# Graph network kernel: 832 record gathers move from the loop ahead of attention into the attention stage

## What is computed

```
edge_index = jnp.stack([src, dst])
x = _layernorm(x + _L0_gnn_ref(x, edge_index, ...))                  # attention over the edges, 4 heads
x = _layernorm(x + _L1_gnn_ref(x, node_vec1, W, b, edge_index))      # masked, degree-weighted sums
x = _layernorm(x + _L2_gnn_ref(x, edge_weight, edge_attr_3, ...))    # radial, equivariant messages
x = _layernorm(x + _L3_gnn_ref(x, edge_index, W1, b1, W2, b2))       # two graph convolutions
```

## Time and profile before

| | us |
|---|---|
| median of 3 runs (20086.42 to 20103.31) | 20091.59 |
| span of the profiled execution | 25995.0 |
| the profiled execution's own time | not in the page |
| DVE busy in the span | 16714.1 (64%) |
| POOL busy in the span | 13429.9 (52%) |
| PE busy in the span | 9853.2 (38%) |
| ACT busy in the span | 6288.5 (24%) |

### The profile page before, as it was taken

How to read it: one execution, slowest core, us unless ns; L and a number is a source line. 1 busy time by engine, 2 the same in 40 slices (tenths; PEclk the granted TensorE clock), 3 DMA queues, 4 the chain that set the end, 5 groups by cost and what they waited for, 6 DMA issues and landing times.

```text
span 25995.0 us, 290953 instructions
## 1 busy us (share of the span) xinstructions
PE 9853.2 (38%) x63545; PEld 7350.7 (28%) x63546; DVE 16714.1 (64%) x23622; ACT 6288.5 (24%) x13799; POOL 13429.9 (52%) x14067
## 2 busy tenths in 40 slices
PE   0131000000000006765225666666666666324422
PEld 0131000000000006664223444444444444313421
DVE  9898574547344438888555666666666677555555
ACT  0002121112111105543002333333333345201400
POOL 0187676667777760000664555555555552363165
PEclk6555555555555559985556777777777776555555
DMA  1133434441000001116222000000000006424623
GB/s 14 25 33 27 29 31 29 29 29 13 6 6 6 6 15 48 41 52 227 69 69 18 9 10 9 9 9 9 9 9 9 9 10 144 137 64 87 205 65 61
DMA packets 1751558, 1095.98 MB, mean 42 GB/s; under 512 B 1217323, under 2 KB 1658124, under 8 KB 1750028
## 3 DMA queue, kind: packets, MB, share of 16 engines
q0 software_dynamic: 454272, 412.11, 13.3%
q1 hardware_dynamic: 1089532, 417.46, 6.8%
q10 hardware_dynamic: 207632, 265.14, 3.3%
HBM read 700.94 MB, written 391.12 MB: 42 GB/s over the span
## 4 chain that ended last, share of the span: by engine, by line
DVE 31%; another core or an unknown queue 21%; issue 17%; DVEq 12%; PE 11%; ACT 4%; DMA 2%; ACTq 1%; POOL 0%; SPq 0%; POOLq 0%
PE banks L1423 5%; DVE arena L1768 5%; DVE arena L1767 4%; DVE red L2523 4%; DVEq L2201 3%; DVE hot L2196 2%; DVE arena L1740 2%; DVE arena L2207 2%; DVE srcs L2516 2%; PE banks L1365 2%; PE banks L1410 2%; DVEq L498 1%; DVE arena L1585 1%; DVEq L2261 1%
## 5 line engine op out<-in xcount | busy, mean ns | idle before, releaser
L804 POOL DMA_INDIRECT srcs<-spread,nbx x2808 | 2653.2, 945 | 5691.9 <-issue 3372.8
L782 POOL DMA_INDIRECT gat<-tab,nbr x3328 | 3455.0, 1038 | 2537.8 <-issue 1271.9
L1423 PE MATMUL banks<-w2rows,dsts 128*128 128x384 f32 x6656 | 3443.8, 660 | 1030.2 <-DVE srcs L2516 699.0
L782 POOL DMA_INDIRECT gat<-tab,pay x3328 | 3161.6, 950 | 1077.4 <-issue 892.0
L748 POOL DMA_INDIRECT pay<-records,nbr x2560 | 2746.2, 1073 | 843.1 <-issue 827.1
L1208 PE MATMUL banks<-ident,arena 128*128 128x128 f32 x2240 | 436.2, 379 | 7154.4 <-DVE arena L1768 2837.8
L909 ACT COPY banks<-arena 128x1024 f32<-128x1024 f32 (+1 forms) x1508 | 1318.6, 875 | 6430.8 <-issue 2701.9
L2511 DVE TENSOR_TENSOR srcs<-banks,g_s 128x512 f32<-128x512 f32 x1664 | 1146.1, 689 | 2252.6 <-remote 1505.1
L1208 PEld LDWEIGHTS banks<-ident,arena 128*128 128x128 f32 x2240 | 400.7, 204 | 7190.5 <-DVE arena L1768 2844.2
L2523 DVE TENSOR_REDUCE red<-srcs 128x160 f32<-128x2560 f32 x832 | 2346.2, 2820 | 75.6
L1279 PE MATMUL banks<-srcs,hot 128*128 128x96 bf16 (+1 forms) x11232 | 1169.8, 281 | 3175.7 <-DVE hot L2196 2136.8
(11 more groups left out here) (392 smaller groups left out, 22029.8 us busy)
## 6 DMA issues: line engine op xcount, KB each, us to landing
spread<-srcs SPq DMA_DIRECT2D x936, 192.0 KB, 2.9
dsts<-key_rows SPq DMA_DIRECT2D x234, 512.0 KB, 4.1
spread<-srcs ACTq DMA_DIRECT2D x468, 204.0 KB, 2.4
staged<-gat SPq DMA_DIRECT2D x416, 148.0 KB
gat<-staged ACTq DMA_DIRECT2D x416, 148.0 KB, 2.1
dsts<-key_rows ACTq DMA_DIRECT2D x117, 512.0 KB, 4.3
gat<-tab,nbr POOLq DMA_INDIRECT x3328
gat<-tab,pay POOLq DMA_INDIRECT x3328
```

Of the source, the lines that this page charges most:

```text
L782: pool.indirect_dma_start(out=gatv(s, GC[pas])[:, t, :], out_offset=None, in_=TAB[pas], in_offset=bass.IndirectOffsetOnAxis(ap=row, axis=0 ...
L804: pool.indirect_dma_start(out=chunk_rows(s, c)[:, q, :], out_offset=None, in_=rows, in_offset=bass.IndirectOffsetOnAxis(ap=nbx[:, r, s * X ...
L1423: last = t_.matmul(bank[1 + 2 * (p % 2) + h][:, 0:384], hid_rows[:, s % 2, 2 * p + h, :], w2rows[:, :], start=True, stop=True)
```

## The change

POOL's first record loop covers 54 rounds instead of 80 (`EARLY_ITERS` = 54, 1728 gathers). The next 26 rounds (`MID_ITERS`, 832 gathers) are made by a new loop, `mid_records`, of 104 rounds with four steps, two gathers a step, into the small buffer `late`. Each pair waits for its indices, for its slot and for the logits of the attention step with its number. SP has a loop of its own for them, `mid_loads`. The counts behind them are raised to match; the radial layer takes the same 24 rounds as before.

```
+MID_ITERS = 26
+MID_TILES = 2
+READY_ITERS = ITERS - LATE_ITERS
+EARLY_ITERS = READY_ITERS - MID_ITERS
...
+            def mid_round(i, first, final):
+                for s in range(SLOTS):
+                    if not first:
+                        sp.wait_ge(rec_in[s], i * (16 * MID_TILES) + 16 * TPS * EARLY_ITERS)
+                        sp.dma_start(by_dst_v[:, mid_tiles(i - 1, s), :], late[:, s, :, :]).then_inc(rec_out[s], 16)
+                    if not final:
+                        sp.dma_start(nbr[:, s, 0:MID_TILES], ids_dst[:, mid_tiles(i, s)]).then_inc(nbr_in[s], 16)
+
+            def mid_loads():
+                mid_round(0, True, False)
+                with sp.Fori(1, ITERS) as i:
+                    mid_round(i, False, False)
+                mid_round(ITERS, False, True)
...
             record_loads()
+            mid_loads()
             chunk_number_loads(PASS_L1, from_dst)
             send_table(1, tab2, F)
             for s in range(SLOTS):
-                sp.wait_ge(rec_out[s], 16 * EARLY_ITERS)
+                sp.wait_ge(rec_out[s], 16 * (EARLY_ITERS + ITERS))
             edge_loads()
...
+            def mid_records():
+
+                def step(i, s):
+                    pool.wait_ge(nbr_in[s], nbr_count(1, EARLY_ITERS + i))
+                    pool.wait_ge(rec_out[s], i * 16 + 16 * EARLY_ITERS)
+                    pool.wait_ge(logit_ready, i * SLOTS + (s + 1))
+                    pool.nop(nofuse=True)
+                    for t in range(MID_TILES):
+                        pool.indirect_dma_start(
+                            out=late[:, s, t, :], out_offset=None, in_=records,
+                            in_offset=bass.IndirectOffsetOnAxis(ap=nbr[:, s, t:t + 1], axis=0),
+                        ).then_inc(rec_in[s], 16)
...
             gather(PASS_MAX)
             collect()
+            mid_records()
             chunk_gather(0, PASS_L1, C1, spread[0])
```

More of the change, by code:

```diff
@@ L42 @@
 LATE_ITERS = 24
-EARLY_ITERS = ITERS - LATE_ITERS
+MID_ITERS = 26
+MID_TILES = 2
+READY_ITERS = ITERS - LATE_ITERS
+EARLY_ITERS = READY_ITERS - MID_ITERS
 LATE_TILES = 2
@@ L75 @@
 assert LATE_ROUNDS * LATE_TILES == LATE_ITERS * TPS
-assert EARLY_ITERS < LATE_ROUNDS < ITERS and LATE_ITERS * SLOTS + 1 < LATE_ROUNDS + SLOTS
+assert MID_ITERS * TPS == ITERS * MID_TILES and MID_TILES == LATE_TILES
+assert READY_ITERS < LATE_ROUNDS < ITERS and LATE_ITERS * SLOTS + 1 < LATE_ROUNDS + SLOTS
 assert XROWS * M == CHUNKS * CHUNK_EDGES and QROWS * M == P * NT and XGPS * XTILES == TPS
@@ L599, in record_loads, with mid_tiles @@
                 record_round(EARLY_ITERS, False, True)
+            def mid_tiles(i, s):
+                return bass.ds(i * (SLOTS * MID_TILES) + (EARLY_ITERS * SLOTS * TPS + s * MID_TILES), MID_TILES)
+            def mid_round(i, first, final):
[10 more added lines that the diff above has]
+                mid_round(ITERS, False, True)
             def late_tiles(i, s):
-                return bass.ds(i * (SLOTS * LATE_TILES) + (EARLY_ITERS * SLOTS * TPS + s * LATE_TILES), LATE_TILES)
+                return bass.ds(i * (SLOTS * LATE_TILES) + (READY_ITERS * SLOTS * TPS + s * LATE_TILES), LATE_TILES)
             def edge_round(i, late_store, late_load, first=False, late_step=None):
@@ L608, in edge_round @@
                     if late_step is not None:
-                        due = late_step * 16 + 16 * (EARLY_ITERS + s + 1)
+                        due = late_step * 16 + 16 * (EARLY_ITERS + ITERS + s + 1)
                         if not isinstance(i, int):
@@ L621, in edge_round @@
                     if late_store:
-                        sp.wait_ge(rec_in[s], i * (16 * LATE_TILES) + 16 * TPS * EARLY_ITERS)
+                        sp.wait_ge(rec_in[s], i * (16 * LATE_TILES) + (16 * TPS * EARLY_ITERS + 16 * MID_TILES * ITERS))
                         sp.dma_start(by_dst_v[:, late_tiles(i - 1, s), :], late[:, s, :, :]).then_inc(rec_out[s], 16)
@@ L628, in edge_loads @@
                 edge_round(0, False, True, True)
-                with sp.Fori(1, EARLY_ITERS) as i:
+                with sp.Fori(1, READY_ITERS) as i:
                     edge_round(i, True, True)
-                with sp.Fori(EARLY_ITERS, LATE_ROUNDS) as i:
-                    edge_round(i, True, True, late_step=i * SLOTS - EARLY_ITERS * SLOTS)
-                edge_round(LATE_ROUNDS, True, False, late_step=(LATE_ROUNDS - EARLY_ITERS) * SLOTS)
+                with sp.Fori(READY_ITERS, LATE_ROUNDS) as i:
+                    edge_round(i, True, True, late_step=i * SLOTS - READY_ITERS * SLOTS)
+                edge_round(LATE_ROUNDS, True, False, late_step=(LATE_ROUNDS - READY_ITERS) * SLOTS)
                 with sp.Fori(LATE_ROUNDS + 1, ITERS) as i:
-                    edge_round(i, False, False, late_step=i * SLOTS - EARLY_ITERS * SLOTS)
+                    edge_round(i, False, False, late_step=i * SLOTS - READY_ITERS * SLOTS)
             def neighbour_load(i, s):
@@ L755, in collect @@
                     step(i, False)
+            def mid_records():
[9 more added lines that the diff above has]
+                        ).then_inc(rec_in[s], 16)
+                for s in range(SLOTS):
+                    step(0, s)
+                with pool.Fori(1, ITERS) as i:
+                    for s in range(SLOTS):
+                        step(i, s)
             def late_records(i, s, first):
-                pool.wait_ge(nbr_in[s], nbr_count(1, EARLY_ITERS + i))
-                if not first:
-                    pool.wait_ge(rec_out[s], i * 16 + 16 * EARLY_ITERS)
+                pool.wait_ge(nbr_in[s], nbr_count(1, EARLY_ITERS + ITERS + i))
+                pool.wait_ge(rec_out[s], i * 16 + 16 * (EARLY_ITERS + ITERS))
                 pool.nop(nofuse=True)
```

## The result

The changed kernel takes 20164.53 us (median of 5 runs, 20157.94 to 20171.1) beside 20086.66 us for the kernel before in the same session (5 runs, 20077.45 to 20103.31): a ratio of 1.0039, 95% interval 1.0028 to 1.005. It is slower by 78 us, more than the 0.2% that can be told from no change. The forecast was no change; the time lies inside the range that was given.

What follows compares the result with a forecast made beforehand. The prediction took attention to be bound by DVE, with POOL's record gathers done 458 us before they are wanted. Its terms summed to 0 us on the path, so 20091 us, range 19900 to 20200.

Steps and rivals of the forecast that it cites:

- Are the waits beside gathers in the runs?: DVE's waits beside POOL's gathers in the stretched profile: claimed to be mostly absent from the runs.
- The rivals that held the waits for real: Waits real: attention takes them, 20593 to 20740 us, chance 0.07; or it does not, 19325 to 19500, chance 0.20.
- the sum of 5998 against 5903: Waits before attention, in radial and chunk gather stages: 5998 us, against 5903 us by which the profiled execution exceeds a run.
- The timeline of a run: Start to first chunk gather: attention from 6428, POOL's last record gather at 8520, chunk gathers wanted at 8978.
- 458 us of slack: Before the first chunk gather: POOL is done with its record gathers 458 us before it is wanted.
- 832 gathers behind the logits: 0 us: Moved pairs on POOL's queue: logits always ready, gathers issued at the same moments, ending at 8520; 0 us.
- Loop rounds: 67 us, covered: POOL's new loop: 78 more rounds at 0.86 us, 67 us, covered by the 458 us, of which 391 remain.
- Buffers: 9.0 us against a round of 9.96: A slot's pair in the new loop: 9.0 us until its next pair can follow, within a 9.96 us round; costs nothing.
- The 14.4 us a round: Time per round of the new loop above which POOL would be late for the chunk gathers, wanted at 8978.
- SP and later stages: 0: SP's 832 DMAs take at most 582 us of 1036; the radial stage fetches the same last 24 iterations; 0 us.
- The rival that came true: POOL late for the chunk gathers, small rounds paid: 20159 us, or 20262 at 16 us per round; chance 0.13.
- The profile after: Profiled span of the changed kernel: between 25230 and 26640 us, thought 26300, while the runs stand still.

Runs made afterwards that it cites:

- e1: The kernel before, with no edit, profiled a second time: span 20097.7 us in an execution of 20099.57 us, median of its runs 20082.47 us.
- e2: The changed kernel without POOL's wait for the logits in the moved gathers: 20161.59 us, ratio 1.0044 to the kernel before.
- e5: The changed kernel with the moved gathers in rounds of four tiles a slot, 52 rounds in place of 104: 20079.92 us, ratio 1.0003 to the kernel before.
- e7: The changed kernel with its two record loops in the other order and no wait for the logits: 20104.66 us, ratio 1.0014 to the kernel before.

## Why the prediction was wrong

- **Are the waits beside gathers in the runs?** Right. e1 keeps DVE busy for 4325 of 4541 us beside the neighbour gathers, and attention starts at 6277. The rivals that held the waits for real (20593 to 20740, and 19325 to 19500) had nothing. But the sum of 5998 against 5903 only said that the parts fit as a whole; it was no check of POOL's pace. The rule that records cost no cycles, from which I took what speaks for those rivals ("NOTIFIC — the notification-queue block", section 10, of the Trainium skill), is not contradicted by e1: its profiled execution took 20099.57 us, and the runs beside it 20065.99 to 20101.24. It doesn't explain, and no run here does.
- **The timeline of a run: the step that failed.** "POOL starts at 1189 and needs 5888 x 1.245 = 7331 us: its last record gather is at 8520." It is at 9030, 510 us later. The neighbour gathers took 1.36 us each, not 1.245 (381 us for 3328), the records 1.289 (111 us for 2560), and 17 us lie between the two. I had taken 0.944 us from the radial stage's records, where nothing else uses much of the DMA engines. The row of the stretch itself has 6200.73 us for 5888 gathers: 1.053 each, and with 0.30 between them 1.353; that sum ends at 9156, past the 8978 at which I had the chunks wanted. It is a row of the stretched execution, and in e1 the same gathers are busy for 6030.4 us; but the evidence that there was no cover stood in a row that I had used only for its count. The other end was off as well: attention came at 6277 and not 6428, and DVE was ready at 8787 and not 8978. In place of 458 us of slack there were 250 us of lateness (458 - 510 - 191, and the wait for the chunk numbers).
- **832 gathers behind the logits: 0 us.** Right that the wait never holds (1.2 us; e2). Wrong that the first loop ends at 7484 (7903.5); the pairs met the end of attention and the spread stage, not attention.
- **Loop rounds: 67 us, covered.** Wrong twice: nothing covered them, and they are next to nothing. A turn costs at most 0.14 us (e5), 11 us for 78 of them, and none is to be seen in e7's 500 us. The 0.86 us of the earlier trace rows was one turn in the stretched execution; in e1 the longest idle time of that kind ahead of a record gather is 0.3 us.
- **Buffers: 9.0 us against a round of 9.96.** Right in quiet stretches (177 gathers in 220 us). In the spread stage it was 14.5 us in the turn shown and 12.9 on average, where POOL's own work for a round is 11.1. "The taken value is 9.0, and it costs nothing" is the second step that failed: the landing time of the earlier trace rows was carried into a stage at 226 GB/s. This term, which I held to be nothing, is the 78 us: in that stage POOL is idle for 221.7 us ahead of 445 gathers, 86 us more than the 0.30 us before each; e5 removes it by giving the chain twice the time. The 14.4 us a round at which I had the rival decide counted on the slack; without it every round above POOL's own pace is paid.
- **SP and later stages: 0.** Right: SP's DMA instructions are 0.35 us each, and the radial stage needs 14.1 us a step in both (5874 and 5853 us for 416), against the 14.2 worked out.
- **The rival that came true** is POOL being late for the chunk gathers, at 0.13 and 20159 us; measured 20164.53. Its place is right and its price right by luck: it has the 67 us of loop turns, and the time was lost to landings. Its chance of 0.13 did not reckon with how little it took: 1.245 us a gather where the mean is 1.33, 7% more, used up all of the slack.
- **The profile after.** Wrong: I expected a span near 26300 from a stretched execution, and 20165.4 came.

The Trainium skill's page "SBUF — State Buffer", section "Who interferes with whom", has a DVE instruction with two SBUF inputs contend with a GpSimd instruction that reads SBUF. That bears on the term that failed: beside such instructions gathers took 1.41 us (below). The prediction had asked of them only whether DVE slows, and not whether POOL does.

## What to carry over

Where an engine makes 5888 equal steps, its pace has to be read in the very stretch in which it runs: take the row's own busy time and gap for one step, multiply them out to the end, and only then speak of slack. Where the bound is one in-order queue, moving work within that queue wins nothing; moving it past the instruction that others wait for wins its full length (32 gathers 40 us, 96 gathers 122 us), until the next engine decides (274 us here). And a buffer's round trip must be priced with the landing times of the busiest stage that it will meet; a deeper round (four tiles for two) is cheap insurance.

## What the runs showed of the hardware

**Gathers slow down beside some DVE work.** A stretch of e1 in which DVE is busy without a gap (it counts pairs of windows) and one inside a sort, all engines, and DVE's largest group in the first:

```profile
1400.00:2050.00 650.00, 295.72 (x3016) 265.37 (x3017) 649.70 (x383) 0.00 (x0) 534.47 (x380) 0.50 0.34 24
2400.00:3600.00 1200.00, 117.79 (x640) 112.51 (x640) 1155.80 (x1022) 406.95 (x390) 919.24 (x922) 0.54 0.46 33
```

```profile
L1585 DVE TENSOR_TENSOR arena<-iota,arena 128x1568 bf16<-128x1568 f32 x379 | 645.2, 1781 | 0.1
```

A gather is 534.47/380 = 1.41 us on POOL in the first, 1.71 from start to start. The same gathers take 1.00 us (919.24/922) in the second, where DVE is nearly as busy, its largest groups read PSUM and the DMA share is higher, and those of attention take 0.944 (1300.32/1377). That the operation of the first stretch reads two SBUF tiles agrees with the section named above; PE is busier beside it than in the second, and no run took the operation away to test it. In the spread stage, where DVE's casts read PSUM, gathers are 1.09 us; its DMA share of 0.73 is as likely a reason, and that is open too.

**A small DMA's landing grows two- to threefold under load:** in the turns shown, index loads of 1 KB land after 1.78 us at a DMA share of 0.13 and after 5.50 at 0.76, a pair's data after 2.40 and 6.25. Over the landings that stand in the chain of the changed kernel the medians are 1.73 and 4.67 us for indices (34 and 50 of them), 2.34 and 4.81 for data (33 and 56). Beside one transfer of 6656 KB an index load took 20.48 us (e7). "DMA: Bandwidth & Descriptors" in the Trainium skill, section "Latency and other measured facts", has the receipt from memory as the largest part of a fixed cost of about 2 us, smaller when the memory is less loaded. The quiet landings agree; the loaded ones are well beyond it.

**One profiled execution can be stretched by 29%** (25995.0 to 20091.59) with rows that look like real waits, while nine others of this program and its variants, the kernel before among them, lie within 3 us of the execution's own time. What stretched it is not known.
